# Routing logits computed the other way round, a tile-wise opening, one attention step a slot later, and block additions tile by tile

## The chip, the cores and the metric

The kernel runs on one core of one Trainium2 chip. The metric is the device time of one execution in microseconds. Below, PE is TensorE, DVE is VectorE, ACT is ScalarE, POOL is GpSimd and SP is SyncE, which here only issues transfers. PE keeps a stationary operand of up to 128 columns (the weight load, PEld) and streams the other operand through it.

## The reference

A block of three layers on 2 x 1024 tokens of width 512, all in float32. The first and the last layer are the same routed feed-forward network, the middle one is gated linear attention in chunks of 64 tokens with four heads.

```python
x = x + 0.5 * ffn(layernorm(x))
x = x + attention(layernorm(x))
x = x + 0.5 * ffn(layernorm(x))

def ffn(x):
    scores = softmax(x @ gate_w.T)              # 64 fine experts
    w_e    = top 8 of scores, the others 0
    flat   = w_e[:, inv_map]                    # 8 groups of 8
    soft   = softmax(where(flat == 0, -1e9, flat))
    xg     = x + soft @ mask_up_w               # per group
    y      = sum over groups of flat.sum * down(silu(gate(xg)) * up(xg))

def attention(x):                               # per head, per chunk
    b = cumsum(logsigmoid(gate)/16);  qe = q*exp(b)*scale;  kd = k*exp(-b)
    o = tril(qe kd^T) v + qe S
    S = exp(b_last)*S + (k*exp(b_last-b))^T v
```

## The kernel before

The 2048 tokens are four blocks of 512, and a block is four tiles of 128 tokens. Each block goes through the feed-forward network twice, so there are eight passes (`PHASES`), in the block order 0, 1, 2, 0, 3, 1, 2, 3. A pass has 22 chunks of 128 inner columns. For each chunk PE computes the gate product into bank `GB` (12 matmuls of 512 columns and one for the routed part, `soft`), the up product into `UB` (the same 13), and in between the down product of the chunk before (`down`, 12 matmuls), which is added up in the four banks `YB` over the pass. Every operand is split into a rounded high part and a low rest (`x_hi`, `x_lo`, `a_hi`, `a_lo`), and each product takes three matmuls.

The order of work is written out by hand. Each chunk has three slots, so a pass has 66 slots, and into them every engine puts the pieces of two other jobs: the attention layer of the block whose first feed-forward pass has just ended (`attention(t, k, q)`, in passes 1, 2, 4 and 5), and the routing of the next pass (`router(p, k)`). On PE slot 3n stands after the gate product of chunk n, slot 3n+1 after its up product, and slot 3n+2 after the down product that follows. Engines meet only through semaphores, and each engine executes its own list in order.

Routing of a pass, by slots: statistics at 28, normalization (`norm`) and PE transposes (`turn`, into bank `W1`; in the opening into the `YB` banks) at 31 to 36, high and low parts (`hi` on ACT, `low` on DVE), logits on PE at 38, softmax and top 8 on ACT and DVE at 38 to 41, a transpose at 43, the permutation at 44, the group softmax at 44 to 46 and the last transposes at 49 to 51. The router weights are `gate_s`: 64 high columns and 64 low columns side by side. The logits were computed for each token tile with the tokens as stationary operand: 4 tiles x 4 parts of the width x (high, low) = 32 matmuls that stream the 128 columns of `gate_s`. ACT then copied the high half of `W1` and DVE added the low half.

Attention, from slot 30: head h takes the six slots from 30 + 6h. The first transposes the key of the head (L1075) and ACT copies it to `k2t`, the second computes the scores (L1082, ACT copies their diagonal blocks to `scm`), the third the state updates (L1088), which DVE adds up in eight steps (`state_of`, L750).

The opening, before pass 0, has no feed-forward work to lie beside. SP issues every first load: the whole of block 0 (`xr(0)`), the constants, the first raw weights, and then ten small loads more. Fifteen of them count on one semaphore, `ld_const`, for which PE, ACT and DVE all wait ahead of their first matmul, their first copy and the first `norm`. In pass 0 ACT and DVE also split the raw weights into high and low parts (`gu_hi`, `gu_lo`, `d_hi`, `d_lo`), the masked routed weights go through `masked`, `m_mask`, `m_top`, `m_rest`, and POOL stores all of it for the later passes.

At the end of a pass, `flush` on DVE adds half of the four `YB` banks to the block, each tile a 128x512 addition, after the last down product as a whole. After the last pass SP stores the four tiles.

## Time and profile before

| | before |
|---|---|
| median of 3 runs | 1925.19 us (1920.02 to 1925.96) |
| the profiled execution, its own time | 1923.59 us |
| its span, first to last instruction | 1921.9 us |
| PE busy | 1871.7 us, 97% |
| DVE, ACT, POOL busy | 781.9, 507.0, 134.1 us |
| idle time of PE before the first matmul | 18.2 us |

A row of a timeline gives start, length, engine, source line, operation, output and inputs, and in square brackets the time that the engine had been idle and what ended it. PE's matmuls overlap, so the pace is read from start to start, not from a length. A float32 matmul of unsplit operands stands as two rows of the trace (x8 for four instructions). A row of a window table gives busy time and number of instructions of each engine, then the clock granted to TensorE, the busy share of the transfer engines and GB/s.

### The profile page before, as it was taken

What the parts mean: (1) busy time and instruction counts of PE and PEld (TensorE: products, weight loads), DVE (VectorE), ACT (ScalarE), POOL (GpSimd) and SP (SyncE); (2) the same over time, 40 slices, a digit from 0 to 9 for tenths busy, and PEclk for the clock granted to TensorE, in tenths of its full rate; (3) what the DMA queues carried; (4) which work ended last, traced back from release to release, by engine and by line L of the source; (5) the groups of instructions that cost most, each with busy time, mean ns of one, the idle gap of its engine ahead of it and who ended that gap; (6) DMA issues with size and microseconds to landing.
All of it is one profiled execution on the core that took longest, in us unless ns stands there. A gap on an engine that the chain in (4) does not pass through costs nothing.

```text
span 1921.9 us, 23031 instructions
## 1 busy us (share of the span) xinstructions
PE 1871.7 (97%) x9024; PEld 1564.9 (81%) x9024; DVE 781.9 (41%) x1464; ACT 507.0 (26%) x780; POOL 134.1 (7%) x231
## 2 busy tenths in 40 slices
PE   4899999999999999999999999999999999999998
PEld 3778787888888888888888888888888888888887
DVE  4456644454343454323424455343454323423222
ACT  2333421343213332111311343213332111311111
POOL 0012110010000100000001010000100000000000
PEclk9899999999999999999999999999999999999999
DMA  4798876555575644576567564575644576567664
GB/s 146 250 352 330 296 285 255 191 191 170 174 249 186 211 165 165 193 242 230 203 222 271 192 216 171 170 249 186 211 165 165 195 245 233 198 220 253 222 238 162
DMA packets 95099, 416.38 MB, mean 217 GB/s; under 512 B 11760, under 2 KB 12144, under 8 KB 67984
## 3 DMA queue, kind: packets, MB, share of 16 engines
q1 hardware_dynamic: 56416, 291.29, 42.6%
q0 software_dynamic: 12336, 77.34, 10.3%
q10 hardware_dynamic: 26240, 46.28, 8.9%
q8 instruction: 73, 1.20, 0.2%
q14 instruction: 34, 0.28, 0.0%
HBM read 365.71 MB, written 49.15 MB: 216 GB/s over the span
## 4 chain that ended last, share of the span: by engine, by line
PE 91%; DVE 3%; ACT 2%; DMA 2%; issue 1%; SPq 1%; ACTq 0%; DVEq 0%
PE bank L932 26%; PE bank L934 26%; PE bank L933 26%; PE bank L1153 4%; PE bank L942 1%; PE bank L964 1%; PE bank L963 1%; PE bank L1082 1%; PE bank L1096 1%; DMA wt<-scr_w 1%; PE bank L1095 1%; PE bank L1088 1%; DMA b_all<-wgu 1%; DVE act_t L608 1%; PE bank L987 0%
## 5 line engine op out<-in xcount | busy, mean ns | idle before, releaser
L932 PE MATMUL bank<-x_hi,wt 128*128 128x512 f32 x1408 | 558.2, 396 | 4.1 <-DMA wt<-scr_w 2.7
L934 PE MATMUL bank<-x_lo,wt 128*128 128x512 f32 x1408 | 550.8, 391 | 0.0
L933 PE MATMUL bank<-x_hi,wt 128*128 128x512 f32 x1408 | 550.4, 391 | 0.0
L608 DVE TENSOR_TENSOR act_t<-bank,sig 128x512 f32<-128x512 f32 x176 | 121.6, 691 | 645.7 <-PE bank L1153 636.5
L932 PEld LDWEIGHTS bank<-x_hi,wt 128*128 128x128 f32 x1408 | 265.8, 189 | 57.5 <-DMA wt<-scr_w 3.6
L934 PEld LDWEIGHTS bank<-x_lo,wt 128*128 128x128 f32 x1408 | 265.3, 188 | 57.1
L933 PEld LDWEIGHTS bank<-x_hi,wt 128*128 128x128 f32 x1408 | 265.7, 189 | 52.3
L932 PE MATMUL bank<-dt,a_hi 128*128 128x512 f32 x704 | 279.5, 397 | 0.3 <-DVE a_lo L608 0.3
L934 PE MATMUL bank<-dt,a_hi 128*128 128x512 f32 x704 | 275.1, 391 | 0.0
L933 PE MATMUL bank<-dt,a_lo 128*128 128x512 f32 x704 | 274.3, 390 | 0.0
L561 ACT ACTIVATE sig<-bank 128x512 f32<-128x512 f32 x176 | 105.3, 598 | 503.2 <-PE bank L1153 503.2
L392 ACT ACTIVATE a_hi<-act_t 128x512 fp32r<-128x512 f32 x176 | 111.0, 631 | 373.5 <-DVE act_t L608 373.0
L608 DVE TENSOR_TENSOR a_lo<-act_t,a_hi 128x512 fp32r<-128x512 f32 x176 | 121.5, 690 | 156.8 <-ACT a_hi L392 156.7
L934 PEld LDWEIGHTS bank<-dt,a_hi 128*128 128x128 f32 x704 | 132.1, 188 | 28.5
L932 PEld LDWEIGHTS bank<-dt,a_hi 128*128 128x128 f32 x704 | 132.5, 188 | 26.5 <-issue 0.7
L933 PEld LDWEIGHTS bank<-dt,a_lo 128*128 128x128 f32 x704 | 132.4, 188 | 26.0
L1153 PE MATMUL bank<-softT,wt 128*128 128x512 f32 x352 | 139.0, 396 | 7.7 <-DVE wt L608 6.9
L608 DVE TENSOR_TENSOR act_t<-s_bc,act_t 128x512 f32<-128x512 f32 x176 | 121.9, 692 | 6.8 <-DMA s_bc<-scr_s 0.9
L1153 PEld LDWEIGHTS bank<-softT,wt 128*128 128x128 f32 x352 | 66.3, 189 | 25.4 <-DVE wt L608 10.8
L608 DVE TENSOR_TENSOR x_lo<-bank,x_hi 128x512 fp32r<-128x512 f32 x48 | 33.1, 689 | 51.1 <-ACT x_hi L392 51.1
L942 PE MATMUL bank<-ident,o_all 128*128 128x128 f32 x192 | 30.7, 286 | 19.9 <-DVE o_all L659 19.9
L932 PE MATMUL bank<-x_hi,tw 128*128 128x512 f32 x128 | 49.8, 389 | 0.0
(166 smaller groups left out, 1752.0 us busy)
## 6 DMA issues: line engine op xcount, KB each, us to landing
wt<-scr_w SPq DMA_DIRECT2D x154, 1152.0 KB, 5.2
dt<-scr_d SPq DMA_DIRECT2D x154, 512.0 KB, 5.2
s_bc<-scr_s ACTq DMA_DIRECT2D x128, 256.0 KB, 5.3
tw<-scr_t POOLq DMA_DIRECT2D x28, 1024.0 KB, 5.3
scr_w<-wt POOLq DMA_DIRECT2D x22, 1152.0 KB, 8.4
b_all<-wgu SPq DMA_DIRECT2D x22, 512.0 KB, 7.6
scr_d<-dt POOLq DMA_DIRECT2D x22, 512.0 KB, 6.1
scr_t<-tw POOLq DMA_DIRECT2D x7, 1024.0 KB, 7.7
```

The costliest lines, as they stand in the source:

```text
L392: return nc.scalar.activation(dst, src, ACT.Copy)
L561: nc.scalar.activation(sig[:], GB[:], ACT.Silu).then_inc(sig_ok, 1)
L608: return nc.vector.tensor_tensor(dst, a, b, op)
L932: mm(dst, wh, xh, start=start, stop=False)
L933: mm(dst, wl, xh, start=False, stop=False)
L934: return mm(dst, wh, xl, start=False, stop=stop)
L942: ins = nc.tensor.transpose(b[:, cols(k)], xn[:, i % 2, cols(k)], ident[:])
L963: mm(W1[:, cols(i)], x_hi[:, s, kk, cols(i)], gate_s[:, kk, :], start=(kk == 0), stop=False)
L964: ins = mm(W1[:, cols(i)], x_lo[:, s, kk, cols(i)], gate_s[:, kk, :], start=False, stop=(kk == KC - 1))
L1082: ins = mm(W0[:, cols(i)], b_all[:, h, cols(i)], q_all[:, h, cols(i)], start=True, stop=True)
L1088: ins = mm(W0[:, cols(i)], k2t[:, i, :], vtz[:, i, h, :, :], start=True, stop=True)
L1153: return mm(b[:], m[:, c0:c0 + P], softT[:, p % 2, c % 2, :], start=False, stop=True)
```

## The change

Four edits. (1) The logits are turned: `gate_s` is stationary and the 512 tokens stream through it, 8 matmuls of 512 columns. The result has high and low logits in rows 0 to 63 and 64 to 127; ACT copies all of it (`lgT`), and four float32 matmuls against `fold_m` (two identity matrices one above the other) turn it back and add the halves, one slot later (39). DVE reads the sum from the bank; ACT's exponential moves from slot 39 to slot 40. (2) The opening: block 0 comes in four transfers with a semaphore each; five constants are issued by ACT with own semaphores and ten more by ACT in the middle of the opening; the decay weights are prepared in chunk 1 of pass 0; the logits stand ahead of `masked(0)`, and the softmax of the opening ahead of `m_mask(0)` on DVE. (3) Of head 0, the scores move from slot 31 to 32 and the update from 32 to 33. (4) `flush` waits for each tile's last down product (`y_ok`) instead of for all four.

```diff
+        lgT = tb_flat[:, 3 * NT * E + NT * 2 * P + NB:3 * NT * E + NT * 2 * P + 2 * NB]
-        N_CONST = 15
+        N_CONST = 10
+        def step_of(k):
+            return {31: 5, 32: 1, 33: 2}.get(k, (k - 30) % 6)
# SP
-            sp.dma_start(xr(0), x_t[0]).then_inc(ld_x[0], 16)
-            sp.dma_start(ident[:], c_id).then_inc(ld_const, 16)
...
+            for i in range(NT):
+                sp.dma_start(xr(0)[:, i, :], x_t[0][:, i, :]).then_inc(ld_x0[i], 16)
# ACT, routing
-                    copy(r_a, W1[:].rearrange("p (t c) -> p t c", t=NT)[:, :, 0:E]).then_inc(logit_cp, 1)
-                elif k == 39:
+                    copy(lgT, W1[:]).then_inc(logit_cp, 1)
+                elif k == 40:
# ACT, opening
-            act.wait_ge(ld_const, 16 * N_CONST)
-            copy(gate_s[:, :, 0:E], raw_gate)
...
+            act.dma_start(ident[:], c_id).then_inc(ld_id, 16)
+            act.dma_start(raw_gate, w_gate).then_inc(ld_gate, 16)
+            act.dma_start(raw_mup.rearrange("p k h e -> p k (h e)"), w_mup).then_inc(ld_mup, 16)
+            act.dma_start(perm_i[:], inv.partition_broadcast(E)).then_inc(ld_perm, 16)
+            act.dma_start(iota[:], c_iota).then_inc(ld_perm, 16)
+            router(0, 32)
+            router(0, 33)
+            act.wait_ge(ld_gate, 16)
+            copy(gate_s[:, :, 0:E], raw_gate).then_inc(gate_hi_ok, 1)
+            router(0, 35)
+            router(0, 36)
...
             gu_hi(0)
+            gu_hi(1)
+            act.dma_start(raw_k1, w_gk1).then_inc(ld_const, 16)
+            for r in range(6):
+                act.dma_start(raw_k2[r * LOW:(r + 1) * LOW, :], w_gk2).then_inc(ld_const, 16)
+            act.dma_start(reset[:], c_reset).then_inc(ld_const, 16)
+            act.dma_start(bias[:], bgk).then_inc(ld_const, 16)
+            act.dma_start(wn[:], wnorm.partition_broadcast(P)).then_inc(ld_const, 16)
+            for k in range(37, 43):
                 router(0, k)
# ACT and DVE, pass 0
+                    if n == 1:
+                        decay_weights()      # on DVE: decay_rests()
# DVE, routing
-                elif k == 38:
-                    dve.wait_ge(logit_cp, p + 1)
-                    step(tt(r_a, W1[:].rearrange("p (t c) -> p t c", t=NT)[:, :, E:2 * E], r_a, ALU.add))
-                    step(nc.vector.tensor_reduce(mx, r_a, AX.X, ALU.max))
+                elif k == 39:
+                    dve.wait_ge(folded, p + 1)
+                    step(nc.vector.tensor_reduce(mx, logits, AX.X, ALU.max))
# DVE, end of a pass
-                dve.wait_ge(d_used, (p + 1) * CH)
                 for i in range(NT):
+                    if i + 1 < NT:
+                        dve.wait_ge(y_ok, p * (NT - 1) + i + 1)
+                    else:
+                        dve.wait_ge(d_used, (p + 1) * CH)
# PE, routing
                 elif k == 38:
                     pe.wait_ge(x_lo_ok, (r + 1) * NT)
-                    for i in range(NT):
-                        for kk in range(KC):
-                            mm(W1[:, cols(i)], x_hi[:, s, kk, cols(i)], gate_s[:, kk, :], start=(kk == 0), stop=False)
-                            ins = mm(W1[:, cols(i)], x_lo[:, s, kk, cols(i)], gate_s[:, kk, :], start=False, stop=(kk == KC - 1))
+                    for kk in range(KC):
+                        mm(W1[:], gate_s[:, kk, :], x_hi[:, s, kk, :], start=(kk == 0), stop=False)
+                        ins = mm(W1[:], gate_s[:, kk, :], x_lo[:, s, kk, :], start=False, stop=(kk == KC - 1))
+                    ins.then_inc(logit_ok, 1)
+                elif k == 39:
+                    pe.wait_ge(logit_cp, p + 1)
+                    for i in range(NT):
+                        ins = mm(W1[:, cols(i, E)], lgT[:, cols(i)], fold_m[:], start=True, stop=True)
+                    ins.then_inc(folded, 1)
# PE, opening
-            pe.wait_ge(ld_const, 16 * N_CONST)
+            pe.wait_ge(ld_id, 16)
             for k in range(32, 37):
                 router(0, k)
+            pe.wait_ge(gate_ok, 1)
+            router(0, 38)
             pe.wait_ge(setup_lo, 2)
             masked(0)
-            pe.wait_ge(perm_ok, 4)
-            for k in range(37, 43):
-                router(0, k)
+            pe.wait_ge(fold_ok, 1)
+            router(0, 39)
             main(GB, 0, 0, 0)
             main(UB, P, 0, 0)
+            pe.wait_ge(perm_ok, 4)
```

**ACT in the opening.** This is ACT's list from its first copy on. `state` is where the raw router and mask weights are loaded, `og` holds the mask weights, `wt<-b_all` is `gu_hi`. Before:

```order
L392 ACTIVATE gate_s<-state 128x4x64
L392 ACTIVATE k_s<-state 128x16x16
L392 ACTIVATE gk_s<-k2t 128x512
L392 ACTIVATE og<-state 128x4x96 x2
L392 ACTIVATE wt<-b_all 128x1024
L392 ACTIVATE x_hi<-bank 128x4x128 x4
L392 ACTIVATE wt<-b_all 128x1024
L392 ACTIVATE wt<-gt 128x256
L392 ACTIVATE tb<-bank 128x256
L440 ACTIVATE tb<-tb 128x256
```

And of the changed kernel:

```order
L395 ACTIVATE x_hi<-bank 128x4x128 x2
L395 ACTIVATE gate_s<-state 128x4x64
L395 ACTIVATE x_hi<-bank 128x4x128 x2
L395 ACTIVATE og<-state 128x4x96 x2
L395 ACTIVATE wt<-b_all 128x1024 x2
L595 DMA state<-w_gk 128x64
L597 DMA k2t<-w_gk 16x512 x6
L598 DMA reset<-c_reset 128x512
L599 DMA bias<-bgk 128x4
L600 DMA wn<-wnorm 128x64
L395 ACTIVATE tb<-bank 128x512
L443 ACTIVATE tb<-tb 128x256
```

The copies of the block (`x_hi`) now come first, the two copies for the decay weights (`k_s`, `gk_s`) are gone from here, and ten transfers are issued right ahead of the copy of the logits (`tb<-bank`).

**PE at slots 31 and 32 of the first attention.** L1153 ends the up product, `dt,a_hi` is the down product. Before, the scores (L1082) stand between the two:

```order
L933 MATMUL bank<-x_hi,wt 128x512
L934 MATMUL bank<-x_lo,wt 128x512
L1153 MATMUL bank<-softT,wt 128x512
L1082 MATMUL bank<-q_all,b_all 128x128 x4
L932 MATMUL bank<-dt,a_hi 128x512
```

In the changed kernel (scores L1140) they stand behind the twelve matmuls of the down product, ahead of the router's transposes (L993):

```order
L984 MATMUL bank<-dt,a_lo 128x512
L985 MATMUL bank<-dt,a_hi 128x512
L1140 MATMUL bank<-q_all,b_all 128x128 x4
L993 MATMUL bank<-ident,o_all 128x128 x4
L983 MATMUL bank<-x_hi,wt 128x512
```

So the scores move behind one down product; the updates move by a slot too, from behind that down product to behind the next gate product.

**DVE at slots 32 and 33 of the first attention.** `act_t` are the gating products of a chunk, `state`/`carry` the eight steps of `state_of`, `x_lo` and `o_all` the router's `low` and `norm`. Before:

```order
L608 TENSOR_TENSOR a_lo<-act_t,a_hi 128x512
L744 MEMSET state 128x64
L750 SCALAR_TENSOR_TENSOR state<-state,dec,bank 128x64 x7
L750 SCALAR_TENSOR_TENSOR carry<-state,dec,bank 128x64
L608 TENSOR_TENSOR x_lo<-bank,x_hi 128x4x128
L659 TENSOR_SCALAR o_all<-x_res,mv,rstd 128x512
L608 TENSOR_TENSOR x_lo<-bank,x_hi 128x4x128
L659 TENSOR_SCALAR o_all<-x_res,mv,rstd 128x512
```

And of the changed kernel:

```order
L632 TENSOR_TENSOR a_lo<-act_t,a_hi 128x512
L632 TENSOR_TENSOR x_lo<-bank,x_hi 128x4x128
L683 TENSOR_SCALAR o_all<-x_res,mv,rstd 128x512
L770 MEMSET state 128x64
L776 SCALAR_TENSOR_TENSOR state<-state,dec,bank 128x64 x7
L776 SCALAR_TENSOR_TENSOR carry<-state,dec,bank 128x64
L632 TENSOR_TENSOR x_lo<-bank,x_hi 128x4x128
L683 TENSOR_SCALAR o_all<-x_res,mv,rstd 128x512
```

The first `low` and `norm` of the router pass the eight steps, the second pair stays behind them.

## Rows read from the trace of the kernel before

**Rows 1.** The page's busy times.
```profile
PE 1871.7 (97%) x9024; PEld 1564.9 (81%) x9024; DVE 781.9 (41%) x1464; ACT 507.0 (26%) x780; POOL 134.1 (7%) x231
```

**Rows 2.** Waits of PE, whole span: us in total, times, longest.
```profile
PE bank L1153 <- DVE wt L608: 6.9, 8, 2.0
...
PE bank L1082 <- ACT k2t L392: 3.9, 4, 1.0
```

**Rows 3.** Timeline of the opening.
```profile
0.80 0.44 SPq L250 DMA_DIRECT2D x_res<-x  x1
...
6.46 0.69 DVE L651 BATCH_NORM_STATS2 stats<-x_res 128x6 f32<-128x512 f32 x1 [6.46 <-DMA x_res<-x]
...
7.64 3.24 SPq L261 DMA_DIRECT2D k2t<-w_gk  x6
7.86 0.57 POOL L299 TENSOR_TENSOR rstd<-ve,mhalf 128x1 f32<-128x1 f32 x1
...
16.68 0.42 ACT L392 ACTIVATE gate_s<-state 128x256 fp32r<-128x256 f32 x1 [14.60 <-DMA wn<-wnorm]
...
18.23 1.94 PE L942 MATMUL bank<-ident,o_all 128*128 128x128 f32 x8 [18.23 <-DVE o_all L659]
...
22.32 0.54 DVE L659 TENSOR_SCALAR o_all<-x_res,mv,rstd 128x512 f32<-128x512 f32 x1
...
24.07 0.60 ACT L392 ACTIVATE x_hi<-bank 128x512 fp32r<-128x512 f32 x1 [0.46 <-PE bank L942]
24.56 1.05 ACT L392 ACTIVATE wt<-b_all 128x1024 fp32r<-128x1024 f32 x1
24.70 0.69 DVE L608 TENSOR_TENSOR x_lo<-bank,x_hi 128x512 fp32r<-128x512 f32 x1 [0.36 <-ACT x_hi L392]
...
28.51 0.31 PE L963 MATMUL bank<-gate_s,x_hi 128*128 128x128 f32 x1
...
35.23 0.73 PE L932 MATMUL bank<-x_hi,wt 128*128 128x512 f32 x1
...
41.93 0.60 PE L969 MATMUL bank<-ident,tb 128*64 128x128 f32 x4
...
53.35 1.19 PE L1153 MATMUL bank<-softT,wt 128*128 128x512 f32 x2 [0.72 <-issue]
```

**Rows 4.** Three windows: span; PE, PEld, DVE, ACT, POOL; clock, transfer share, GB/s.
```profile
57.70:61.60 3.90, 3.90 (x9) 3.09 (x10) 2.25 (x4) 1.15 (x2) 0.00 (x0) 0.50 0.42 78
...
65.00:100.00 35.00, 34.87 (x168) 28.98 (x167) 17.98 (x25) 11.13 (x18) 3.71 (x7) 1.00 0.96 356
...
105.90:109.20 3.30, 3.30 (x10) 2.55 (x9) 1.23 (x1) 0.68 (x1) 0.00 (x0) 0.51 0.98 322
```

**Rows 5.** Timeline of PE: the logits for pass 1, first row, and what surrounds them.
```profile
183.59 0.39 PE L934 MATMUL bank<-dt,a_hi 128*128 128x512 f32 x1
183.82 0.22 PE L963 MATMUL bank<-gate_s,x_hi 128*128 128x128 f32 x1
...
187.34 0.34 PE L1140 MATMUL bank<-wt,og 128*128 128x256 f32 x1
```

**Rows 6.** Timeline of PE: the permutation (four matmuls of 64 columns), and what follows.
```profile
467.09 1.10 PE L974 MATMUL bank<-perm,tb 64*128 64x64 f32 x8
468.13 0.50 PE L932 MATMUL bank<-x_hi,wt 128*128 128x512 f32 x1
```

**Rows 7.** Timeline of the first attention, slot 31.
```profile
414.78 0.59 ACT L392 ACTIVATE k2t<-bank 128x512 f32<-128x512 f32 x1
...
415.43 1.16 PE L1082 MATMUL bank<-q_all,b_all 128*128 128x128 f32 x8 [0.96 <-ACT k2t L392]
```

**Rows 8.** Timeline of the end of the program.
```profile
1916.59 2.48 DVE L851 SCALAR_TENSOR_TENSOR x_res<-bank,x_res 128x512 f32<-128x512 f32 x4 [3.15 <-PE bank L934]
1917.31 2.13 SPq L287 DMA_DIRECT2D out<-x_res  x4
```

**Rows 9.** Transfers of one tile of a block: KB each, median us to landing.
```profile
out<-x_res SPq DMA_DIRECT2D x4, 256.0 KB, 2.2
```

117 lines of the change are left out of this document (70 added, 47 removed).

## The prediction, made before the changed kernel had run

> **What bounds the kernel now.** I read the page's busy times first: PE is busy 97% of the span, the next engine 41% [rows 1]. So time can come out of three places only: PE's own work, the holes in PE's work, and the stretches before the first and after the last matmul. The list of PE's waits shows few holes: four of about 1.0 us for the copy `k2t`, and eight, 6.9 us in all, for the masked weights of pass 0 [rows 2]. The large hole is the opening. In its timeline the first block has landed at 6.46 us, but ACT's first copy starts at 16.68 after 14.60 us of idling, ended by the landing of `wn`, the last constant of the shared semaphore, and PE's first matmul at 18.23 [rows 3]. From there the opening is a chain through all engines up to the first routed product at 53.35 [rows 3], where pass 0 begins. Behind the last matmul stand four additions, the stores and their landing: from 1916.59 to the end of the span at 1921.9 [rows 8].
>
> **Turned logits.** At full pace the 32 matmuls take from 183.82 to 187.34, 3.52 us or 0.110 us each, while a 512-column matmul takes 0.23 us from start to start [rows 5]. Streaming 128 columns thus costs half of streaming 512. The new product is 8 x 0.23 = 1.84 us. The fold is not in the trace. Its nearest row is the permutation: four float32 matmuls, also 64 columns streamed against a 128-column stationary operand, 467.09 to 468.13, 1.04 us [rows 6]. Its bounds are 0 and the time of as many transposes twice over, about 2 x 1.0 us (eight transposes take 1.94 us at half pace [rows 3]); I take 1.04. Each routing saves 3.52 - 1.84 - 1.04 = 0.64 us, seven of them 4.5 us (bounds -2.2 and +11.8). This PE time has no cover, so it counts in full. Also by the Trainium skill, "TensorE: Matmul & The Clock Gate", section "Back-to-back issue gap", a stream of weight loads and matmuls costs about 81 ns at 128 columns and 131 ns at 512. By it a routing would save 32 x 0.081 - 8 x 0.131 - 1.04 = 0.5 us, an estimate from that page, seven of them 3.5 us; the trace's paces of 110 and 230 ns are higher than both, and the sum goes by the trace.
>
> The new waits of this edit: the fold waits for ACT's copy of 512 columns, 0.60 us [rows 3], and between logits and fold PE has 13 matmuls of the gate product, 13 x 0.23 = 3.0 us. DVE waits for the fold at slot 39, with nothing queued behind it but the gating of the next chunk, which needs the up product that PE only starts after the fold. The exponential at slot 40 goes behind ACT's copies of the attention output; the transpose that needs its result stands at slot 43, one down product, one gate and one up product later, 12 + 13 + 13 matmuls or 8.7 us. I cost both at 0; without this cover each would cost its excess in each of seven passes.
>
> **Scores a slot later.** PE waited 0.96 us for `k2t` [rows 7], four times 3.9 us in all [rows 2]. The scores now stand behind a down product of 12 x 0.23 = 2.8 us, more than the wait, so all 3.9 us go. What is late next: the update and DVE's eight steps come one slot later, and the next key transpose that needs the state stands three slots after that, about 8 us. Behind the steps on DVE are one `low` and one `norm`, 0.69 + 0.54 us [rows 3], and then a gating. No wait is added. Bounds 0 and 3.9.
>
> **Additions tile by tile.** PE never waits for `flush` within the run, since the first down product of a pass comes a chunk later, so seven of eight flushes are worth 0. At the end, three of the four additions, which take 2.48 us together [rows 8], now lie under the last down product: 3/4 x 2.48 = 1.9 us. The stores were issued within 2.13 us right behind them [rows 8] and one lands in 2.2 us [rows 9]; the last one's issue moves forward by the same 1.9 us. I take 1.8 (bounds 1.4 and 2.1).
>
> **The opening.** Here I follow the chain, with lengths from rows 3. A tile of 256 KB lands in 2.2 us when alone [rows 9]; block 0 as one 1 MB transfer took from 0.80 to 6.46. I put the four tiles at 3.5, 4.5, 5.5 and 6.6 us. Statistics of tile 0 (0.69, and 0.2 that I allow to aggregate) end at 4.4, POOL's two steps (0.57, and 0.25 allowed for the smaller) at 5.5, `norm` 0.54 at 6.1; PE's four transposes take 1.94/2 = 1.0 us. From here DVE is the pacer: it has three more tiles of statistics (0.9 each), three more `norm` (0.54), four `low` (0.69) and the low half of `gate_s` (0.42, as ACT's copy), about 7.3 us, which ends at 13.4. The logits, eight 512-column matmuls at half pace (0.43 us each, as the 32 took (35.23 - 28.51)/32 = 0.21), run from 13.4 to 16.9. ACT in the meantime: last `x_hi` at 12.7, `og` 0.9, two `gu_hi` of 1.05, so 15.8. Then it issues ten transfers; SP needed 3.24 us for six such [rows 3], so ten take about 5.2, and only at 21.0 does ACT copy the logits (0.60). `masked(0)`, eight matmuls of 256 columns at half of 0.43 us, 1.7 us, has covered PE up to 18.7; then PE is idle for 3 us. This is a new wait, about 3.5 us of ACT's time in the chain. Fold 21.7 to 22.7. The main products of chunk 0 took 41.93 - 35.23 = 6.7 us, so the transpose of the weights could start at 29.4; DVE's softmax and top 8 took no longer than those same 6.7 us before, from the end of the logits at 35.23 to the transpose that needs them at 41.93, so they do not bind later than PE. From that transpose to pass 0 it took 53.35 - 41.93 = 11.4 us, and nothing in this part changes except that 0.4 us of `m_rest` on DVE lies under ACT's exponential. So pass 0 starts at about 41, or 12.4 us earlier.
>
> Two prices are open here. One is PE's pace in the main products. After an idle stretch a stretch of nine matmuls ran at a granted clock of 0.50, the 1.2 GHz level, from 57.70, and one in pass 0 at 0.51, from 105.90 [rows 4]. If the 3 us of idling keep the whole of the 24 matmuls at 0.43 us, they take 10.3 instead of 6.7, and the gain is 8.8. The other is ACT's issue time: if ten issues cost ACT nothing, the gain is 15.9. I take 12.0, a little under the sum, for the first.
>
> **Rest of pass 0.** Its transfers are started by compute, with the transfer engines 96% busy in 65 to 100 [rows 4], so the pass should shift as a whole. Four instructions of at most 0.60 or 0.69 us enter chunk 1, where PE has waited for DVE's masked weights [rows 2]: 0 to 1.4 us lost, I take 0.3.
>
> **Sum.** 4.5 + 3.9 + 1.8 + 12.0 - 0.3 = 21.9 us. The profiled execution, 1921.9 us of span and 1923.59 in its own time, comes to 1901.7. The median of the runs is 1.6 us above that execution, which would give 1903.3. I predict 1902.5.
>
> **Rivals.** (a) *The opening gives half.* Tiles land later than I put them, or the half clock holds, or the ACT issues cost more. For it: the transfers of ident, gate and mask weights, 320 KB, now run beside the tiles; with 1 MB in 5.66 us that is 1.8 us for the last tile, and with the slow clock 12.0 becomes 7. Result 1907.5. The Trainium skill, "DMA: Bandwidth & Descriptors", section "Issuing engines are not separate DMA queues", says that transfers started by different engines share the same 16 DMA engines and interleave, and that starting them from several saves only the time to issue; it speaks for this rival, and no row here shows two queues loading side by side in an idle machine. Chance 0.25. (b) *The opening gives more*, 16 us, because the issues on ACT don't hold it up or the first tiles land before 3.5: 1898.5. Against it, SP's rows show 0.54 us per such issue [rows 3]. Chance 0.15. (c) *Pass 0 swallows the gain.* The transfer engines are 96% busy there [rows 4]. The earlier start shifts the transfers with the compute, but the changed order in chunk 1 can make raw weights land later than they did, and a wait like the longest of 2.0 us [rows 2], with a stretch at half clock behind it, twice or three times costs about 10 us: 1912. Against it, PE was busy 34.87 of 35 us in that window. Chance 0.07. (d) *Slower.* The fold at slot 39 waits for ACT in each of seven passes. A wait of 2 us also costs a stretch at half clock, 3.3 us long [rows 4], half of it lost, 1.65: 3.65 us per pass, 26 in all, which turns -21.9 into +4 (1928, or 1929 by the median). It decides from (21.9 + 5.8)/7 = 4.0 us per pass for more than 0.3% slower. Against it, the cover of 3.0 us over 0.6. Chance 0.03, of which half within 0.3%. (e) *Turned logits save nothing*, because the fold costs 2 us: 1909. Chance 0.06. The forecast itself, 1899 to 1906, has 0.44.
>
> **How the numbers follow.** Leaving out (c), (d) and the far part of (b) gives 1895 to 1911. What a measurement of this kernel can tell from no change is about 0.3%, 5.8 us. All cases but (d) and a tail of (c) and (a) are faster by more: faster 0.94, same 0.04, slower 0.02.
>
> **What would show it.** The first matmul near 6 us; ten issues on ACT between about 16 and 21 with PE idle up to the fold; the first routed product near 41; eight 512-column logits at 0.23 us and a fold of about 1.0 us in seven passes; no waits for `k2t`; one addition behind the last matmul. The prediction is wrong if the opening ends after 47, or if PE shows waits at slots 33, 39 or 43 that were not there.

## The result: 1.4% faster, and the profile after

| | before, beside it | changed |
|---|---|---|
| median, 4 runs each | 1923.72 us (1920.02 to 1925.96) | 1896.12 us (1893.99 to 1896.5) |
| ratio | | 0.9862 (95% interval 0.984 to 0.9883) |
| the profiled execution, its own time | 1923.59 us | 1896.5 us |
| its span | 1921.9 us | 1894.6 us |

The kernel is faster by 1.4% (1.2 to 1.6%). 1902.5 us was predicted, with a range of 1895 to 1911. The median lies in it, near its lower end. The two spans differ by 27.3 us where the sum had 21.9.

The page's busy times after. PE has 128 instructions fewer than in [rows 1] and is busy 10.8 us less; the rest of the 27.3 us is idle time that has gone.
```profile
PE 1860.9 (98%) x8896; PEld 1551.6 (82%) x8896; DVE 777.8 (41%) x1457; ACT 508.5 (27%) x780; POOL 131.8 (7%) x231
```

The waits of PE after, whole span: us in total, times, longest. They answer to [rows 2].
```profile
PE bank L993 <- DVE o_all L683: 9.9, 7, 6.5
PE bank L1211 <- DVE wt L632: 7.5, 9, 2.0
...
PE bank L983 <- DMA wt<-scr_w: 1.2, 2, 1.1
```

Two rows of the same view of the kernel before, which [rows 2] do not show:
```profile
PE bank L942 <- DVE o_all L659: 19.9, 2, 18.2
...
PE bank L932 <- DMA wt<-scr_w: 2.7, 2, 1.9
```

The waits for `k2t` are gone from the list. The masked weights of pass 0 are waited for as before, 7.5 us against 6.9. L993 (L942 before) is the transpose of the normalized tiles. Before, it waited twice, both times in the opening. Now it waits seven times: 6.5 us before the first matmul, twice more in the opening, and four times about 0.44 us in the attention passes, where before there was no wait. `wt<-scr_w` are weights that pass 0 stored and a later pass loads back. All these come up again below.

The timeline of the opening after: start, length, engine, line, operation, and idle time before. It answers to [rows 3].
```profile
3.73 0.69 DVE L675 BATCH_NORM_STATS2 stats<-x_res 128x6 f32<-128x512 f32 x1 [3.73 <-DMA x_res<-x]
...
6.50 1.09 PE L993 MATMUL bank<-ident,o_all 128*128 128x128 f32 x4 [6.50 <-DVE o_all L683]
...
7.06 0.69 DVE L675 BATCH_NORM_STATS2 stats<-x_res 128x6 f32<-128x512 f32 x1 [0.71 <-DMA x_res<-x]
...
13.93 1.04 ACT L395 ACTIVATE wt<-b_all 128x1024 fp32r<-128x1024 f32 x1
14.08 0.76 PE L1013 MATMUL bank<-x_hi,gate_s 128*128 128x512 f32 x1 [1.50 <-DVE x_lo L632]
...
15.24 1.85 ACTq L597 DMA_DIRECT2D k2t<-w_gk  x4
...
17.63 0.40 PE L1198 MATMUL bank<-wt,og 128*128 128x256 f32 x1
...
18.59 0.60 ACT L395 ACTIVATE tb<-bank 128x512 f32<-128x512 f32 x1 [2.66 <-PE bank L1014]
...
19.33 1.08 PE L1020 MATMUL bank<-fold_m,tb 128*128 128x64 f32 x8 [0.48 <-ACT tb L395]
...
20.21 0.48 PE L983 MATMUL bank<-x_hi,wt 128*128 128x512 f32 x1
...
25.79 0.60 PE L1025 MATMUL bank<-ident,tb 128*64 128x128 f32 x4
...
37.20 1.19 PE L1211 MATMUL bank<-softT,wt 128*128 128x512 f32 x2 [0.72 <-issue]
```

Read it link by link. The first tile's statistics start at 3.73, PE's first transpose at 6.50, the logits at 14.08, their copy on ACT at 18.59, the fold at 19.33, the main products at 20.21, the transpose of the weights at 25.79, and pass 0 at 37.20 where it was 53.35. ACT's ten issues (the row at 15.24 is four of them) run from 13.92 to 18.5, beside its own `gu_hi` at 13.93 and not behind it.

The same marks in both traces split the 27.3 us with nothing left over (starts of matmuls; "routed product, pass 1" is the routed product of the gate product of chunk 3 in pass 1):

```
mark                         before    changed   gained in the stretch
first routed product          53.35     37.20    16.15   opening
routed product, pass 1       312.99    294.80     2.04   pass 0 and its one routing
last matmul                 1916.16   1890.90     7.07   six routings, four attentions
end of the span             1921.9    1894.6      2.0    tail
```

Two stretches repeat with the same length in every pass and give the price of one routing and one attention. From the routed product of chunk 12's gate product to that of chunk 13's up product, where routing has its logits and fold, it took 15.64 us before and 14.87 after in passes without attention, 17.93 and 17.17 with it: 0.76 to 0.77 us less, and 0.72 in pass 0; seven times, 5.3 us. From chunk 9's up product to chunk 11's up product in an attention pass it took 27.25 before and 26.5 after: 0.74 us less, four times, 3.0 us. Six routings and four attentions are then 7.5 us of a measured 7.07. The other 0.4 us is one place in this execution: at chunk 3 of pass 4 PE waits for weights loaded back,
```profile
1008.63 0.50 PE L983 MATMUL bank<-x_hi,wt 128*128 128x512 f32 x1 [0.16 <-DMA wt<-scr_w]
```
and the stretch around it takes 7.05 us, where the trace of before has 6.64.

One routing lies in pass 0, so all else between the second and the third mark gained 1.3 us. None of it was gained in pass 0 itself. From its first routed product to that of pass 1 it took 229.50 us before and 229.20 after, which is one routing less 0.4 us. The rest was gained in the first three chunks of pass 1, from the first routed product to the third mark: 30.14 us before and 28.40 after, because the waits for `wt<-scr_w` there were shorter.

The routing in pass 1 after, on PE:
```profile
168.09 0.40 PE L1013 MATMUL bank<-x_hi,gate_s 128*128 128x512 f32 x1
...
173.68 0.40 PE L1211 MATMUL bank<-softT,wt 128*128 128x512 f32 x1
173.91 1.00 PE L1020 MATMUL bank<-fold_m,tb 128*128 128x64 f32 x8
174.73 0.48 PE L983 MATMUL bank<-x_hi,wt 128*128 128x512 f32 x1
```

The fold has no bracket, so PE did not wait for ACT's copy, and 0.82 us after it started the next product starts.

The tail after:
```profile
1890.90 0.39 PE L985 MATMUL bank<-dt,a_hi 128*128 128x512 f32 x1
...
1889.32 2.69 DVE L880 SCALAR_TENSOR_TENSOR x_res<-bank,x_res 128x512 f32<-128x512 f32 x4 [1.19 <-PE bank L985]
1890.04 2.33 SPq L288 DMA_DIRECT2D out<-x_res  x4
```

The first addition starts 1.58 us ahead of the last matmul, where it started 0.43 us behind it [rows 8]: (1916.59 - 1916.16) + 1.58 = 2.0 us earlier.

### The profile page after: what moved, and what is told of

Its sections match the earlier page's. It is cut to its first block, busy times and chain, and to the rows that moved or that the text cites. A ratio compares the mean times of both kernels' runs of the same rounds, so it can differ in the third digit from the quotient of the medians.

```text
span 1894.6 us, 22779 instructions
## 1 busy us (share of the span) xinstructions
PE 1860.9 (98%) x8896; PEld 1551.6 (82%) x8896; DVE 777.8 (41%) x1457; ACT 508.5 (27%) x780; POOL 131.8 (7%) x231
## 4 chain that ended last, share of the span: by engine, by line
PE 90%; DVE 4%; DMA 3%; ACT 2%; issue 1%; ACTq 0%; SPq 0%; DVEq 0%
PE bank L983 26%; PE bank L985 26%; PE bank L984 26%; PE bank L1211 4%; DMA wt<-scr_w 1%; PE bank L993 1%; DVE act_t L632 1%; DMA b_all<-wgu 1%; PE bank L1154 1%; PE bank L1153 1%; PE bank L1146 1%; PE bank L1140 1%; PE bank L1043 0%; PE bank L1030 0%; PE bank L1020 0%
## 5 line engine op out<-in xcount | busy, mean ns | idle before, releaser
L1211 PEld LDWEIGHTS bank<-softT,wt 128*128 128x128 f32 x352 | 66.2, 188 | 26.4 <-DVE wt L632 11.8
L983 PE MATMUL bank<-x_hi,tw 128*128 128x512 f32 x128 | 49.8, 389 | 0.0
L984 PE MATMUL bank<-x_hi,tw 128*128 128x512 f32 x128 | 49.8, 389 | 0.0
```

The costliest lines, as they stand in the source:

```text
L983: mm(dst, wh, xh, start=start, stop=False)
L984: mm(dst, wl, xh, start=False, stop=False)
L1211: return mm(b[:], m[:, c0:c0 + P], softT[:, p % 2, c % 2, :], start=False, stop=True)
```

## The experiments

Two theories stood against each other for each part that had a doubt. For the opening: A, ten issues hold ACT up (the prediction's working), against B, they run beside ACT's activations and the gain lies in the earlier first tile. For the routing: the fold costs about 1.0 us and no wait is hidden in it, against a dear fold whose cost a cheaper product pays for. For the attention: whether the scores a slot later give the full 3.9 us. For pass 0, which here is read together with the start of pass 1, from the first routed product to the mark in pass 1: whether it passes a gain in the opening on, or gives part of it back. Every time below stands beside runs of the kernel before on the same chip. Beside the kernels that are timed in several runs it had a median of 1921.26 us, unless another is named.

**The changed kernel again**, on another chip, for what a comparison can tell.

> The changed kernel unaltered, once more, for the spread of its marks between executions. Theory: outside the opening's first 7 us and pass 0 every mark repeats within 0.2 us (steps of 0.76 us at each routing, 0.74 us at each attention against before), while pass 0 differs by one or two quanta of some 1.4 us, the stretches at half pace; ratio to before 0.985 to 0.988. Rival (the stretches in pass 0 are fixed by the program): the same stretches at the same chunks, first at chunk 0 only, then at the start of pass 1.

It took 1896.16 us (1893.72 to 1897.44) against 1922.53, ratio 0.9854 (0.9831 to 0.9878); its span was 1895.5. The routing and attention stretches were 17.17, 14.87 and 26.5 us again, the first routed product came at 37.46 against 37.20, and the tail was 3.7 in both. Pass 0 was the part that differed: 258.57 us from the first routed product to the mark in pass 1, against 257.60. Here PE did not wait for `wt<-scr_w` at all: the first three chunks of pass 1 took 26.81 us instead of 28.40, and pass 0 itself 231.76 instead of 229.20. Those three chunks took 26.81 us in all eleven traces without that wait; the three with it are those of before, of the changed kernel and of the old logits in all passes.

Four of the trials below (step order, `flush`, fold twice, `norm` earlier) also leave the opening and pass 0 of the changed kernel as they are. Over these six executions the first routed product comes between 36.99 and 38.42, and the stretch from there to the mark in pass 1 takes 255.95 to 258.57 us, with 0.9 us taken off for the second fold. So the routing and attention stretches can be read to 0.1 us from one trace, but the opening only to 1.4 us and pass 0 to 2.6 us.

**Old opening, the other three edits kept.** The opening of before, with the turned logits and the fold in it.

```diff
-            for i in range(NT):
-                sp.dma_start(xr(0)[:, i, :], x_t[0][:, i, :]).then_inc(ld_x0[i], 16)
+            sp.dma_start(xr(0), x_t[0]).then_inc(ld_x[0], 16)
+            sp.dma_start(ident[:], c_id).then_inc(ld_const, 16)
...
-        N_CONST = 10
+        N_CONST = 15
```

> The kernel before with the three other edits (turned logits, scores a slot later, additions tile by tile), its opening as it was but for the turned logits and the fold. Theory: the opening as a whole gave 16.2 us, of which the turned logits alone give some 3 us even behind the old loads (logits 3.5 instead of 6.7 us, a faster pair of main products), so about 13 us stay lost: 1909 us, first matmul near 18.3, first routed product near 50. Rival (the loads are only part and the new order of work gives as much): below 1905 us, first routed product below 46.

1906.73 us (1905.86 to 1907.39), ratio 0.9928 (0.9913 to 0.9943). Its ACT and PE begin like this:
```profile
15.77 0.42 ACT L398 ACTIVATE gate_s<-state 128x256 fp32r<-128x256 f32 x1 [13.69 <-DMA wn<-wnorm]
...
17.45 1.94 PE L954 MATMUL bank<-ident,o_all 128*128 128x128 f32 x8 [17.45 <-DVE o_all L665]
```

ACT waits for `wn` as in [rows 3], and the first routed product comes at 49.04. So 53.35 - 49.04 = 4.3 us of the opening's gain came with the turned logits, and 49.04 - 37.20 = 11.8 us with the order of loads and work (10.6 to 12.1 by the six executions). By the median the run was 14.5 us faster than the kernel before beside it, where the changed kernel was 27.6 and 26.4 us faster than its own, so 12 to 13 us were lost. By the span it was only 9.5: pass 0 was 1.9 us shorter here (255.69 us) than in the changed kernel's trace, of which 1.6 us are the wait at the start of pass 1 that this execution did not have.

**Old logits in all passes, all else as changed.**

```diff
+                        for i in range(NT):
+                            for kk in range(KC):
+                                mm(W1[:, cols(i)], x_hi[:, s, kk, cols(i)], gate_s[:, kk, :], start=(kk == 0), stop=False)
+                                ins = mm(W1[:, cols(i)], x_lo[:, s, kk, cols(i)], gate_s[:, kk, :], start=False, stop=(kk == KC - 1))
```

> The changed kernel with the old form of the logits in all eight passes (32 matmuls of 128 columns, no fold). Theory: each of seven routings loses 0.76 us, 5.3 in all, and the opening loses 3 to 4 us, since streams of 128 columns keep PE at half pace: 1905 us. Rival (the seven steps seen between the traces come from something else, the moved exponential or DVE's one addition less): less than 2 us lost outside the opening.

1906.02 us (1904.72 to 1910.87), ratio 0.9929 (0.9914 to 0.9944). The routing stretches were 17.93 and 15.64 again, those of before, so the 0.76 us belong to the turned product and its fold, and not to the moved exponential, which stayed at slot 40. The first routed product came at 41.68, 4.5 us later than in the changed kernel's trace and 3.3 us later than the latest of the six.

**Old logits in the opening alone.** The branch above for pass 0 only.

> The changed kernel with the old logits (32 matmuls of 128 columns) in the opening alone. Theory: streams of 128 columns leave PE at half pace, so the logits take 6.8 instead of 3.55 us, the masked product 1.7 instead of 1.0 and the main pair 6.7 instead of 5.6; no fold (1.4 us with its wait): first routed product near 40.5 instead of 37.2. Rival (PE's pace follows the time since work began, not what is streamed): full pace from about 17.5 on here too, first routed product below 39.

One execution, 1895.6 us (before beside it 1921.37). The first routed product came at 40.35, near the expected 40.5. PE in the opening of this kernel:
```profile
14.52 0.44 PE L1024 MATMUL bank<-gate_s,x_hi 128*128 128x128 f32 x1 [1.50 <-DVE x_lo L636]
...
21.38 0.52 PE L1213 MATMUL bank<-wt,og 128*128 128x256 f32 x1
...
23.19 0.63 PE L992 MATMUL bank<-x_hi,wt 128*128 128x512 f32 x1
23.61 0.46 PE L993 MATMUL bank<-x_hi,wt 128*128 128x512 f32 x1
23.91 0.39 PE L994 MATMUL bank<-x_lo,wt 128*128 128x512 f32 x1
24.14 0.40 PE L992 MATMUL bank<-x_hi,wt 128*128 128x512 f32 x1
```

The 128-column matmuls ran 0.21 us apart, and so did the 256-column ones, which is half their pace of 0.12 in the changed kernel, and only between 23.61 and 23.91 does the distance of the 512-column ones fall from 0.42 to 0.23, some 9 us after PE's idle end at 14.52. In the changed kernel the 512-column logits start at 14.08 with 0.43 us between them, and from 17.98 on, 3.9 us in, the 256-column matmuls are 0.12 us apart, which is full pace. That point moves from one execution to the next: 2.9 to 6.0 us behind the start of the logits in the six executions. With 128-column logits it was 9.2 us in this one and in that of before, and 12.1 us with the old logits in all passes.

The whole kernel was no longer than the changed one, because pass 0 was 3.5 us shorter (254.07 us). Of that, 1.6 us are again the missing wait at the start of pass 1. The other 1.9 us are in pass 0 itself; one place is ACT's wait for the raw weights of chunk 5, 2.0 us here and 3.8 in the changed kernel. Whether a gain in the opening is given back in pass 0 is not shown by this one execution.

**The step order of the first head undone.**

```diff
-            return {31: 5, 32: 1, 33: 2}.get(k, (k - 30) % 6)
+            return (k - 30) % 6
```

> The changed kernel with the scores and the update of head 0 back at slots 31 and 32. Theory: the waits of 0.96 us for k2t return in four passes and the waits of 0.44 us for o_all at the router's first transposes go: 3.0 us slower, 1899 us. Rival (the predicted 3.9 us went whole, the 0.44 us waits have another cause and stay): 3.9 us slower, waits of 0.44 us still there.

1899.31 us (1895.71 to 1900.8), ratio 0.9887 (0.9872 to 0.9902). The waits of PE of this kernel:
```profile
PE bank L993 <- DVE o_all L683: 8.5, 2, 6.6
...
PE bank L1140 <- ACT k2t L395: 3.9, 4, 1.0
```

Four waits for `k2t`, 3.9 us, come back as in [rows 2], and of the seven waits at L993 five are gone. The attention stretch is 27.25 again: 0.74 us each, not 0.96. (Its median is 3.2 us above the changed kernel's, which says little by itself: its last matmul was only 0.7 us later, mostly because PE did not wait at the start of pass 1, and its last store happened to land late, 5.8 us from the last matmul to the end instead of 3.7. The stretches are the evidence.)

**`flush` waits for all four tiles.**

```diff
+                dve.wait_ge(d_used, (p + 1) * CH)
                 for i in range(NT):
-                    if i + 1 < NT:
-                        dve.wait_ge(y_ok, p * (NT - 1) + i + 1)
-                    else:
-                        dve.wait_ge(d_used, (p + 1) * CH)
```

> The changed kernel with the four additions of a pass waiting for the last down product as a whole. Theory: only the end of the program changes, 1.9 to 2.0 us slower (1898 us). Rival (earlier additions also help the statistics and stores inside the run): over 3 us slower, with new waits of PE within the passes.

1898.79 us (1894.91 to 1899.46), ratio 0.9882 (0.9866 to 0.9899), span 2.1 us longer. Its last matmul starts at 1890.88, as in the changed kernel. Behind it:
```profile
1891.38 2.48 DVE L877 SCALAR_TENSOR_TENSOR x_res<-bank,x_res 128x512 f32<-128x512 f32 x4 [3.25 <-PE bank L982]
1892.10 2.13 SPq L288 DMA_DIRECT2D out<-x_res  x4
```

Additions and issues are 2.06 us later than in the changed kernel, and that is the whole difference. The seven earlier flushes are worth nothing, as predicted.

**The ten late loads issued by SP.** The ten issues leave ACT and go to SP, behind the first raw weights.

```diff
+            sp.dma_start(raw_k1, w_gk1).then_inc(ld_const, 16)
+            for r in range(6):
+                sp.dma_start(raw_k2[r * LOW:(r + 1) * LOW, :], w_gk2).then_inc(ld_const, 16)
...
-            act.dma_start(raw_k1, w_gk1).then_inc(ld_const, 16)
-            for r in range(6):
-                act.dma_start(raw_k2[r * LOW:(r + 1) * LOW, :], w_gk2).then_inc(ld_const, 16)
```

> The changed kernel with the ten late loads issued by SP behind the raw weights instead of by ACT. Theory: ACT issues them while it computes, so its copy of the logits was late by at most 0.5 us: first routed product 36.7 to 37.3. Rival (the recorded prediction, 3.5 us of ACT's time in the chain): first routed product near 34.

One execution, 1897.74 us (before beside it 1921.37). The timeline of its opening:
```profile
17.80 0.60 ACT L401 ACTIVATE tb<-bank 128x512 f32<-128x512 f32 x1 [1.95 <-PE bank L1014]
...
19.27 1.21 PE L1020 MATMUL bank<-fold_m,tb 128*128 128x64 f32 x8
```

With no issue on ACT the copy starts at 17.80, straight behind the last logit, and 0.8 us ahead of the changed kernel's 18.59. So ten issues cost ACT 0.8 us, a little more than the 0.5 expected, where the working had some 3.5. The cost is not the same each time: from the end of the last logit to the copy it took 0.8 us in the changed kernel's trace, 0.2 in the repeated one and 1.6 in the last trial below. And that 0.8 us was worth nothing: in this execution the 256-column product stayed at half pace to its end, so PE reached the fold at 19.27 (changed: 19.33), and the first routed product came at 37.27.

**The five first constants issued by SP behind the tiles.**

```diff
+            sp.dma_start(ident[:], c_id).then_inc(ld_id, 16)
+            sp.dma_start(raw_gate, w_gate).then_inc(ld_gate, 16)
...
-            act.dma_start(ident[:], c_id).then_inc(ld_id, 16)
-            act.dma_start(raw_gate, w_gate).then_inc(ld_gate, 16)
```

> The changed kernel with the five first constants issued by SP behind the four tiles instead of by ACT beside them. Theory (transfers of both queues share the same engines): the tiles land earlier, the third tile's statistics start by 6.4 instead of 7.06, and ident lands later, so that the first matmul starts at 6.5 to 7.0; first routed product within 0.5 us of 37.2. Rival (queues are apart): tiles land as before, and only ident and gate are later, first matmul after 7.

One execution, 1894.23 us (before beside it 1921.37).
```profile
6.05 0.69 DVE L675 BATCH_NORM_STATS2 stats<-x_res 128x6 f32<-128x512 f32 x1
6.41 2.17 PE L993 MATMUL bank<-ident,o_all 128*128 128x128 f32 x8 [6.41 <-DMA ident<-c_id]
```

The third tile's statistics start at 6.05 with no wait, against 7.06 behind a wait of 0.71 in the changed kernel's trace, and those of the fourth at 7.32, also with no wait, against 8.34. In all ten traces with the tile-wise opening in which ACT issues the constants, DVE waits 0.5 to 2.2 us in all for the tiles behind the first, and in the two in which SP does it, here and in the last trial, it does not wait. Now PE's first matmul waits for `ident` instead. The first routed product came at 36.49, 0.7 us earlier than in the changed kernel's trace and 0.5 us earlier than in the earliest of the six. That the tiles came earlier agrees with what the Trainium skill says in "DMA: Bandwidth & Descriptors", section "Issuing engines are not separate DMA queues": transfers started by different engines go through the same transfer engines and interleave. The last tile, which rival (a) had put 1.8 us late, had landed by 7.32 here; where its statistics waited for it in other traces, they started at 8.34 to 9.14, so it was at least 1.0 us later.

**The fold done twice** in passes 1 to 7 (the second time it writes the same result again).

```diff
-                    for i in range(NT):
+                    for i in [*range(NT), *(range(NT) if p else ())]:
```

> The changed kernel with the four matmuls of the fold done twice in passes 1 to 7 (the same result written again). Theory: a fold costs 1.0 us of PE's time, as the permutation, so each of the seven steps grows by 0.9 to 1.0 us: 6.3 to 7.3 us longer. Rival (the fold is partly hidden, its weight loads under the streams before it): below 0.6 us each.

One execution, 1903.91 us (before beside it 1921.37). The timeline of PE:
```profile
430.14 1.90 PE L1020 MATMUL bank<-fold_m,tb 128*128 128x64 f32 x16
431.85 0.48 PE L983 MATMUL bank<-x_hi,wt 128*128 128x512 f32 x1
```

The routing stretches are 18.06 and 15.76, 0.89 us more than 17.17 and 14.87. A second fold, right behind the first, thus costs 0.89 us of PE's time, without any cover and without a wait, and I take that as the price of the first. The old product was 3.52 us; 3.52 - 0.76 - 0.89 = 1.87 us for the new one, and the prediction's 8 x 0.23 was 1.84.

**The router's first two `norm` one slot earlier** in attention passes, ahead of that slot's attention work on DVE, to take away the wait at L993.

```diff
-                elif k == 31:
+                elif k == (30 if p - 1 in ATT else 31):
                     norm(r, 0, src)
...
+                if k == 30 and q in ATT:
+                    router(q + 1, k)
```

> The changed kernel with the router's first two norms at slot 30, ahead of DVE's products, in the four attention passes. Theory: the 0.44 us waits of the router's first transposes come from these norms standing behind the gating of chunk 10; they go, nothing takes their place, 1.8 us faster than the changed kernel by the marks outside pass 0. Rival (the norms at slot 30 delay the products, and with them scores and gating): new waits at the scores or at the up product of the next chunk, no gain or a loss.

1893.58 us (1889.49 to 1894.66), ratio 0.9854 (0.9839 to 0.987) against 1920.26. That is 26.7 us faster than before, no more than the changed kernel's 27.6 and 26.4, so the medians show no gain; the stretches do. In slot 32 of the first attention of this kernel:
```profile
400.17 1.06 PE L1142 MATMUL bank<-q_all,b_all 128*128 128x128 f32 x8
...
401.06 0.60 PE L995 MATMUL bank<-ident,o_all 128*128 128x128 f32 x4
```

The same place in the changed kernel:
```profile
398.84 1.06 PE L1140 MATMUL bank<-q_all,b_all 128*128 128x128 f32 x8
...
399.65 1.00 DVE L683 TENSOR_SCALAR o_all<-x_res,mv,rstd 128x512 f32<-128x512 f32 x2
400.34 0.63 PE L993 MATMUL bank<-ident,o_all 128*128 128x128 f32 x4 [0.44 <-DVE o_all L683]
```

In the changed kernel PE has done the scores and finds `norm` only just under way, since on DVE it stands behind a gating. With `norm` a slot earlier the bracket is gone and the attention stretch is 25.87 instead of 26.5: 0.63 us less, four times 2.5 us. A wait of 0.44 in its bracket thus cost 0.63, and the old one of 0.96 cost 27.25 - 25.87 = 1.38, if the order of the steps costs nothing by itself. Part of that surplus can be read from any two rows of matmuls: each lasts 0.39 while the next starts 0.23 behind it, and the bracket counts from the end of the row, so 0.16 us of lost pace stands in no bracket.

**Block 2 loaded in the opening** instead of in chunk 4 of pass 0, where it stood ahead of the raw weights of chunk 5 in SP's list.

```diff
             sp.dma_start(xr(1), x_t[1]).then_inc(ld_x[1], 16)
+            sp.dma_start(xr(2), x_t[2]).then_inc(ld_x[2], 16)
...
-                if c == 4:
-                    sp.dma_start(xr(2), x_t[2]).then_inc(ld_x[2], 16)
```

> The changed kernel with the 1 MB load of block 2 in the opening, behind that of block 1, instead of in chunk 4 of pass 0. Theory: this load stands right ahead of the raw weights of chunk 5, which ACT awaits for 3.8 us; without it that wait is under 1 us, PE's two waits at chunk 5 (1.1 and 2.0 us in the changed kernel) shrink to under 1 us together, and the stretch at half pace behind them goes: pass 0 is 2 to 4 us shorter, about 1893 us. Rival (the stores and other loads fill the transfer engines anyway, so the wait comes at chunk 6 or later): pass 0 as long as before within 1 us.

1890.29 us (1889.79 to 1891.93), ratio 0.9843 (0.9829 to 0.9856) against 1920.26. ACT at the raw weights of chunk 5, first in the changed kernel, then in this one:
```profile
81.36 1.06 ACT L395 ACTIVATE wt<-b_all 128x1024 fp32r<-128x1024 f32 x1 [3.76 <-DMA b_all<-wgu]
```
```profile
77.64 1.06 ACT L394 ACTIVATE wt<-b_all 128x1024 fp32r<-128x1024 f32 x1 [0.95 <-DMA scr_w<-wt]
```

ACT's wait of 3.76 us for the transfer is gone, and pass 0 is 5.2 us shorter (252.38) than in the changed kernel's trace. 1.6 us of that are the wait at the start of pass 1, which ten other traces don't have either, and 3.6 are in pass 0 itself, where PE's two waits at chunk 5, 1.1 and 2.0 us, became one of 0.5. PE's waits for masked weights fall from 7.5 us to 5.5. The shortest of the six executions had 255.95, still 3.6 us more. By the medians the kernel is 30.0 us faster than before, 2.4 to 3.6 us more than the changed one.

The window of 65 to 100 us in the changed kernel (the columns are those of [rows 4]):
```profile
65.00:100.00 35.00, 31.58 (x148) 25.59 (x147) 16.58 (x25) 11.09 (x18) 4.77 (x9) 1.00 0.95 328
```

And with block 2 early:
```profile
65.00:100.00 35.00, 34.14 (x160) 28.03 (x159) 17.55 (x26) 12.56 (x19) 4.76 (x9) 1.00 0.94 337
```

In [rows 4] PE was busy 34.87 us between 65 and 100, but pass 0 began 16.15 us later then, so that was another part of the pass. The same part before is this:
```profile
81.15:116.15 35.00, 32.86 (x148) 26.61 (x147) 16.49 (x25) 10.94 (x17) 4.76 (x9) 0.95 0.97 344
```

PE did 148 matmuls there before and 148 after, and 160 with block 2 early. The transfer share is 0.94 to 0.97 in all of them, so it did not tell. What told is ACT's wait for the one transfer that stood behind a megabyte of block 2.

**The three together**: block 2 early, the five constants on SP, `norm` a slot earlier.

> The changed kernel with three edits: block 2 loaded in the opening, the five constants issued by SP behind the tiles, the norms of the attention passes at slot 30. Theory: the gains add up, 1.8 (norms), 0.7 (opening) and 2 to 4 us (pass 0): 1889 to 1892 us, faster than both kernels. Rival (pass 0 gives the earlier start back in other waits): 1894 us or more.

1888.93 us (1887.44 to 1894.42), ratio 0.9843 (0.9826 to 0.986) against 1920.26: 31.3 us faster than before, where the changed kernel was 27.6 and 26.4 us faster. The two were not timed beside each other, and one of the five times, 1894.42, lies among the changed kernel's. Pass 0 was 251.07 and the attention stretch 25.86, so two of the three edits add up. The third gave nothing here:
```profile
PE bank L994 <- DMA ident<-c_id: 7.2, 1, 7.2
```

```profile
18.73 0.45 ACTq L599 DMA_DIRECT2D wn<-wnorm  x1
19.23 0.60 ACT L399 ACTIVATE tb<-bank 128x512 f32<-128x512 f32 x1 [3.53 <-issue]
```

`ident` landed at 7.20 here against 6.41 in the single trial, and the first routed product came at 37.84, later than the changed kernel's 37.20. The late `ident` was not the cause, for the logits still started at 13.86, 0.2 us ahead of the changed kernel's. ACT's issues ran until 19.18, and the copy of the logits came right behind them at 19.23, against 18.59. The 0.7 us that the constants on SP had won in one execution are not a gain that can be counted on.

## Why the prediction was right, and where its steps were off

The sign and the range held, and the opening was the largest term as forecast. Term by term:

**Turned logits, 4.5 predicted, 5.3 measured.** The mechanism was right and each part was seen: 1.87 us for the product (1.84 reckoned), no wait of PE at slots 39, 40 and 43. The mis-sized term was the fold, 1.04 reckoned from the permutation [rows 6], 0.89 by the fold done twice. The rest is 3.52 - 1.84 - 0.89 = 0.79, and 0.76 was measured. By the paces of the Trainium skill ("TensorE: Matmul & The Clock Gate", section "Back-to-back issue gap") a routing would have saved 0.5 us by the prediction's estimate. The trace's paces, 110 and 230 ns against the page's 81 and 131, were the nearer ones.

**Scores a slot later, 3.9 predicted, 3.0 measured.** The step that failed was "No wait is added". The working followed what stands behind the eight steps on DVE, but not what the router's transposes in the same slot now find: PE comes to L993 before `norm` is done. The size of the old wait was off as well, and the two errors partly cancel: the old wait was worth 1.38 us and not the 0.96 of its bracket, the new one 0.63, and the difference is the 0.74 measured, give or take 0.01. The 1.38 is an estimate, as said above. The step order undone brought the old waits back and took the new ones away; `norm` a slot earlier took the new ones alone away.

**Additions, 1.8 predicted, 2.0 measured.** Right in mechanism. The additions moved by 2.0 us, a little over the 1.9 of three additions.

**Opening, 12.0 predicted, 16.15 measured.** The start of the chain was nearly as worked out: 6.50 for the first matmul against 6.1, logits at 14.08 against 13.4, at half pace as assumed. (Two of its small sums do not come out, POOL's end at 5.5 for 5.2 and DVE's work at 7.3 for 7.5 us; they cancel.) The step that failed was that ten issues "take about 5.2, and only at 21.0 does ACT copy the logits", the "new wait, about 3.5 us of ACT's time". The copy came at 18.59. The issues began at 13.92, beside ACT's activations, and not at 15.8 behind them, and took 4.6 us. The trial without the issues put their cost at 0.8 us. This is 2.4 us of the miss, all of it ahead of the fold. The "3.5" was too large even by the prediction's own chain: without the issues its fold would have waited for `masked(0)` until 18.7, and 21.7 - 18.7 is 3.0. The other part is the main pair, 20.21 to 25.79 or 5.6 us where 6.7 were taken over from before: 1.1 us, since PE was at full pace from the masked product on. The last link, transpose to first routed product, was 11.41 us against 11.4. From 29.4 to 25.79 is 3.6 us (2.5 up to the main products, 1.1 in them); the other 0.5 of the 4.15 missing is what the forecast took off its own chain, 53.35 - 29.4 - 11.4 = 12.55, to come to 12.0. Rival (b), 16 us because the issues on ACT don't hold it up, is what happened in the main; it had a chance of 0.15, and its time of 1898.5 was 2.4 us from the median, nearer than the forecast's 1902.5. That its 16 met the 16.15 so closely is partly luck: the issues did cost 0.8 us, the faster main pair gave 1.1, and between executions the end of the opening moved by 1.4.

**Rest of pass 0, -0.3 predicted, +1.3 measured** (2.04 less one routing of 0.76). Pass 0 itself was 0.4 us longer than one routing less would make it, close to the 0.3 of the forecast. The gain lies behind it, in the waits for `wt<-scr_w` at the start of pass 1: two of 0.8 and 1.9 us before, one of 1.05 after. The prediction's list of PE's waits left that row out, 2.7 us in all, and put nothing in the sum for it. But the six executions differ by 2.6 us over this part, so neither sign is certain, and why that wait is there in three traces and not in eleven stays open.

Rival (c), that pass 0 swallows part of the gain, was not seen in the difference to before. Nor does it follow from the trials: with an opening 11.8 us longer pass 0 itself took 228.88 us, against 229.20 in the changed kernel's trace and 231.76 in the repeated one, and with one 3.15 us longer 227.25. So as far as it can be read, the pass shifted as a whole. ACT's wait for the raw weights of chunk 5 was 2.5 us in the trace of before, 3.8 and 4.0 in the two of the changed kernel, 2.0 with the opening longer by 3.15 and 4.0 with it longer by 11.8, so it does not follow the length of the opening. That this wait was on the path is shown: block 2 loaded earlier removed it and made pass 0 shorter by at least 3.6 us.

**Median.** 1923.59 - 21.9 became 1902.5 in the forecast; the sum was 5.4 us short, 4.15 of them in the opening, 1.6 in pass 0, 0.8 in the routing, 0.2 in the tail, less 0.9 in the attention and the 0.4 of the wait in pass 4. The median was off by 6.4; the last 1.0 is what the forecast added to its sum, 0.8, and the spread between executions.

What stays open: why `ident` lands at 6.4 in one execution and 7.2 in another, why the third tile's statistics start anywhere between 6.43 and 8.01 in the six executions of one opening, and when PE has to wait for weights loaded back.

## What to carry to other kernels

When a wait on the busiest engine is taken away, look at the next instruction that this engine comes to earlier than before, in the same slot, and at what its operand stands behind; here 0.63 of 1.38 us turned up there, and moving two small instructions on the other engine gave it back. In an opening, follow the chain by data and do not add the time of an engine's transfer issues to its activations before a trace has shown that they exclude each other. Before a difference of a microsecond or two in a part of the program is explained, look how much that part differs between executions that are the same there; here it was 0.1 us for a routing, 1.4 for the opening and 2.6 for pass 0. The busy share of the transfer engines did not tell whether a transfer was on the path; the one wait that ended with a transfer, and what stood ahead of it in its queue, did.

## What the runs showed of the hardware that was not expected

- Issues and activations of one engine run side by side: ten issues on ACT from 13.92 to 18.5 us with two 1.04 us activations between 13.93 and 15.92, and a cost to the next activation of 0.8 us. In the trace with all three edits together that cost was 1.6 us.
- PE has slow stretches in pass 0, six to eight 512-column matmuls 0.43 us apart instead of 0.23, at 0.20 us each 1.2 to 1.6 us for a stretch. In the changed kernel's two traces they stand behind waits of 1.4, 2.2 and 2.0 us. Where they come differs between executions of one program: the wait of 2.00 us that ends at 89.69 in one trace had none behind it, and the same wait, which ends at 91.70 in the repeated one, had this, at the lower of the two clock levels (columns as in [rows 4]):

```profile
92.30:94.86 2.56, 2.56 (x8) 2.00 (x7) 0.75 (x1) 1.54 (x2) 0.43 (x1) 0.50 1.00 277
```

- The clock printed for the opening is 1.00, although the eight 512-column logits ran 0.43 us apart:

```profile
14.00:17.40 3.40, 3.32 (x8) 2.67 (x9) 2.88 (x5) 1.92 (x3) 0.00 (x0) 1.00 0.68 196
```

  This is no reading of the clock. The trace holds no record of the granted clock ahead of 17.87 us, and the view prints 1.00 where it has none. From 17.87 on the record says full clock, and from 17.98 on the matmuls keep full pace. It is the same in the old logits of the opening alone (record from 23.75, full pace from 23.91). Ahead of the first record, read the distance from start to start.
- From the last matmul to the end of the span it took 3.7 us in ten of the profiled executions that add tile by tile, and 5.4 and 5.8 us in the two others (old logits in all passes, step order undone), with the same instructions at the same distances.
